# The experts of a mixture layer: every expert for every token, or tokens sorted by expert and gathered back

## The reference, cut to what matters

```python
xn = layernorm(x)
x = x + attn0(xn) + ffn0(xn)          # first layer
xn = layernorm(x)
x = x + attn1(xn) + ffn1(xn)          # second layer

def ffn0(u):                          # a mixture of experts
    s = softmax(u @ centroids.T + expert_biases)         # 16 experts
    topk_vals, topk_idx = top_k(s, 2)
    g = sum(one_hot(topk_idx, 16) * topk_vals)           # 2 of 16 not zero
    routed = sum over e of g[e] * (u @ Wr[e].T + br[e])   # Wr[e] is 256x256
    shared = (u @ (Ws[0] + Ws[1]).T + bs[0] + bs[1]) / 2
    return u + routed + shared
```

## Time and profile before

| | us |
|---|---|
| median of 3 runs (lowest, highest) | 3472.14 (3467.8, 3472.72) |
| the profiled execution, its own time | 3466.49 |
| its span, first to last instruction | 3464.7 |
| of it to the barrier between the phases | 1232.4 |
| of it `phase_b` | 2232.3 |

### The profile page before, as it was taken

One profiled execution on the slowest core, in us unless ns is written; L12 is line 12 of the kernel. 1 busy time (PEld: TensorE's weight loads), 2 busy tenths in 40 slices (PEclk: granted clock), 3 DMA queues, 4 the chain that ended last, 5 costly groups with the idle time before them and its releaser, 6 DMA issues.

```text
span 3464.7 us, 58322 instructions
## 1 busy us (share of the span) xinstructions
PE 3327.1 (96%) x16386; PEld 2701.4 (78%) x16386; DVE 2480.8 (72%) x4709; ACT 1951.3 (56%) x3226; POOL 2359.6 (68%) x2084
## 2 busy tenths in 40 slices
PE   5999999999999969999999999999999999999997
PEld 4877777777777747888888888888888888888886
DVE  6877777777777756766766667667677666776764
ACT  3333333333333347767767777677777777767774
POOL 4666666666666527777777777777777777777776
PEclk9999999999999979999999999999999999999999
DMA  2110011001001032222222222222322222222222
GB/s 78 31 31 28 28 31 31 26 29 31 27 29 31 25 94 59 47 71 63 59 71 56 62 70 50 66 70 46 74 59 59 73 56 60 70 50 66 70 49 53
DMA packets 195099, 180.22 MB, mean 52 GB/s; under 512 B 87955, under 2 KB 155813, under 8 KB 194469
## 3 DMA queue, kind: packets, MB, share of 16 engines
q1 hardware_dynamic: 194980, 179.04, 20.7%
HBM read 77.25 MB, written 34.08 MB: 32 GB/s over the span
## 4 chain that ended last, share of the span: by engine, by line
PE 61%; DMA 1%; ACT 1%; DVE 1%; POOL 1%; issue 0%; SPq 0%; POOLq 0%; ACTq 0%; DVEq 0%
PE psV_b L1342 7%; PE psV_b L1347 7%; PE psS_b L1330 7%; PE psS_b L1329 7%; PE psV_b L1343 7%; PE psN_b L1315 6%; PE psY_b L1270 4%; PE psX_b L1270 4%; PE psY_b L1271 3%; PE psY_b L1272 3%; PE psX_b L1272 3%; PE psX_b L1271 3%; POOL pp_lo_b L1061 1%; PE psN_b L1399 0%; DMA xT_lo<-xT_lo_dram 0%
## 5 line engine op out<-in xcount | busy, mean ns | idle before, releaser
L1061 POOL TENSOR_TENSOR pp_lo_b<-pf_b,pp_hi_b 128x1024 fp32r<-128x1024 f32 x512 | 1227.6, 2398 | 606.6 <-ACT pp_hi_b L1103 518.9
L1206 DVE TENSOR_REDUCE negmax_b<-psN_b 128x2 fp32r<-128x1024 f32 x512 | 627.1, 1225 | 387.8 <-PE psN_b L1315 380.1
L1098 ACT ACTIVATE pf_b<-psS_b 128x1024 f32<-128x1024 f32 x512 | 526.0, 1027 | 239.4 <-PE psS_b L1330 236.2
L692 PE MATMUL psM_a<-wr_hi_a,xt_hi_a 128*128 128x512 f32 x1024 | 439.6, 429 | 48.1 <-DVE acc_a L528 40.1
L1329 PE MATMUL psS_b<-qA_b,kA_b 128*128 128x512 f32 x1024 | 405.6, 396 | 6.3 <-DVE qB_b L1221 4.5
L694 PE MATMUL psM_a<-wr_hi_a,xt_lo_a 128*128 128x512 f32 x1024 | 409.7, 400 | 0.0
L693 PE MATMUL psM_a<-wr_lo_a,xt_hi_a 128*128 128x512 f32 x1024 | 407.8, 398 | 0.0
L1330 PE MATMUL psS_b<-qB_b,kB_b 68*128 68x512 f32 x1024 | 406.4, 397 | 0.0
L1342 PE MATMUL psV_b<-pp_hi_b,vals_hi_b 128*128 128x512 f32 x1024 | 402.9, 393 | 1.4
L1343 PE MATMUL psV_b<-pp_hi_b,vals_lo_b 128*128 128x512 f32 x1024 | 402.3, 393 | 0.0
L1315 PE MATMUL psN_b<-kA_b,qA_b 128*128 128x512 f32 x1024 | 322.8, 396 | 4.8 <-DVE negmax_b L1206 4.1
(11 more groups left out here) (200 smaller groups left out, 7824.1 us busy)
## 6 DMA issues: line engine op xcount, KB each, us to landing
kA_b<-kA_b SPq DMA_DIRECT2D x128, 256.0 KB, 3.2
qB_b<-qA_b SPq DMA_DIRECT2D x128, 256.0 KB, 2.9
inverse_b<-inverse_dram SPq DMA_DIRECT2D x256, 128.0 KB, 3.0
x_a<-x_dram SPq DMA_DIRECT2D x64, 128.0 KB, 2.1
xT_hi_dram<-xrt_hi_a SPq DMA_DIRECT2D x64, 128.0 KB, 2.1
xT_lo_dram<-xrt_lo_a SPq DMA_DIRECT2D x64, 128.0 KB, 2.1
base_dram<-base_a SPq DMA_DIRECT2D x64, 128.0 KB, 1.8
xT_hi<-xT_hi_dram SPq DMA_DIRECT2D x16, 512.0 KB, 4.3
```

The source lines that it names most:

```text
L692: pe.matmul(out, lh, rh, start=start, stop=False)
L1061: pool.tensor_tensor(pp[1][:, c], pf[:, c], pp[0][:, c].bitcast(F32), ALU.subtract).then_inc(pl_pool, 1)
L1098: a.activation(pf[:, c], psS[:], ACT.Exp).then_inc(exp_act, 1)
L1206: v.tensor_reduce(negmax[:, n.slot(2), 2 * c:2 * c + 2], psN[:], AX.X, ALU.max, negate=True).then_inc(mx_dve, 1)
```

## The change

`phase_a` is replaced by three blocks, one after the other, each closed by a barrier. Loops are written out; a unit is now two tiles (U = 2, 32 units), a group four tiles (16 groups). `need` is the wait.

`route`, 38 steps: normalization, routing, hidden layer and the shared expert, whose sum goes to DRAM (`part`). The experts are not multiplied. Instead DVE chooses two experts for each token of a group (`choose`: 15 operations over 4x16 numbers per token row, each waiting for the one before), TensorE counts with matmuls by triangular matrices how many earlier tokens chose the same expert, and DVE turns that into a row number (`settle_places`: 6 operations); `highest` is two more. POOL then writes each normalized tile twice to those rows of a DRAM array by indirect DMA: in every even step, 8 DMAs of 128 rows of 1 KB, in all 128. Every expert has a region of its own there. At the end SP loads 16 positions from SBUF into registers and writes zeros behind each region.

`experts`: 144 jobs of 128 rows, each of one expert, two per turn (72 turns). SP reads from a table where a job begins and loads the rows; TensorE transposes them, reads from the table which expert it is (`value_load`), and does 7 matmuls of 256 columns (one for the bias) with the weights at that place. ACT and DVE split the weights first, then the rows, and take turns in copying the results, which SP stores. POOL meanwhile converts the row numbers, in 30 small operations.

`settle`: per unit POOL gathers the two result rows of each token (4 indirect DMAs, three units ahead); DVE multiplies them by the two gates and adds them to `part`; then comes the second layer's normalization and ffn, and the stores as before.

```diff
+U = 2
+GU = TB // U
+TOP = 2
...
-def phase_a(nc, io, xT_hi, xT_lo, base_dram, early):
+def need(eng, sem, per, n, k):
+    if per * n + k > 0 and n >= 0:
+        eng.wait_ge(sem, per * n + k)
+def route(nc, io, rows, part, region, jobs, kept, raw, raw_in):
...
+        steps = range(-4, NU + 2)
...
+            sp.wait_ge(const_pool, POOL_CONST)
...
+            for r in range(4):
+                sp.wait_ge(sent[r], 16 * TOP * TB * (GN // 4))
+            for e in range(NE):
+                at = sp.value_load(ends_u[0:1, e:e + 1], min_val=0, max_val=NE * region - P)
+                sp.dma_start(rows[bass.ds(at, P), :], zeros[:]).then_inc(ends_in, 16)
...
+        @block.gpsimd
...
+            for v in steps:
+                u = v + 2
+                if 0 <= v < NU:
+                    hidden_low(v, 0)
+                if 0 <= u < NU:
+                    need(g, r_act, 3, u, 2)
+                    need(g, z_dve, 4, u - 2, 1)
+                    g.tensor_tensor(z2[:, u % 2], q2[:, u % 2], in_tiles(qw2_bc[:], U), ALU.mult).then_inc(z_pool, 1)
+                    g.tensor_tensor(sums[:, u % 4, :, FH:FH + 1], sums[:, u % 4, :, FH:FH + 1], eps[:, 4:4 + U].unsqueeze(2),
+                                    ALU.add).then_inc(z_pool, 1)
+                if v % 2 == 0 and 0 <= (v + 4) // 2 < GN:
...
+                    g.tensor_tensor(rstd[:, a % 2, 1], rstd[:, a % 2, 0], power[:, 0, 0:TB], ALU.pow).then_inc(ln_pool, 1)
+                if 0 <= v < NU:
+                    hidden_low(v, 1)
+                q = (v - 2) // 2
+                if v % 2 == 0 and 0 <= q < GN:
+                    need(g, rt_dve, ROUTE, q, ROUTE)
+                    for t in range(TB):
+                        for k in range(TOP):
+                            n = q * TB + t
+                            g.indirect_dma_start(out=rows[:, :], out_offset=bass.IndirectOffsetOnAxis(
+                                ap=kept.place[:, k, n:n + 1], axis=0), in_=xn[:, q % 4, t], in_offset=None).then_inc(sent[q % 4], 16)
+                if 0 <= u < NU:
+                    need(g, z_dve, 4, u, 1)
+                    need(g, z_dve, 4, u - 4, 3)
+                    need(g, z_pool, 3, u, 2)
+                    g.tensor_tensor(roots[:, u % 4].rearrange("p a b -> p (a b)"), sums[:, u % 4].rearrange("p a b -> p (a b)"),
+                                    power[:, 1, 0:U * (FH + 1)], ALU.pow).then_inc(z_pool, 1)
...
+        @block.scalar
...
+            for v in steps:
+                f1, f2, f3 = v + 1, v + 2, v + 3
+                if 0 <= v < NU:
+                    hidden_tanh(v, 0)
...
+                    a.activation(qsb[:, f2 % 2], psR[:, :, 0:D], ACT.Copy).then_inc(r_act, 1)
+                if 0 <= v < NU:
+                    hidden_high(v, 0)
+                if 0 <= f1 < NU:
...
+                    a.activation(qt[0][:, f1 % 2].rearrange("p a b c -> p (a b c)"), psQ[:, 0], ACT.Copy).then_inc(q_act, 1)
+                if 0 <= f3 < NU:
...
+                    a.activation(xt[0][:, f3 % 6].rearrange("p a b c -> p (a b c)"), psT[:, 0], ACT.Copy).then_inc(t_act, 1)
+                if 0 <= v < NU:
+                    hidden_tanh(v, 1)
+                    hidden_high(v, 1)
...
+        @block.vector
...
+            for s in steps:
+                f1, f2, f3 = s + 1, s + 2, s + 3
+                if 0 <= f1 < NU:
+                    need(v, z_pool, 3, f1, 3)
+                    root = roots[:, f1 % 4]
+                    v.scalar_tensor_tensor(out=qs[:, f1 % 4, 0], in0=root[:, :, FH:FH + 1].to_broadcast([P, U, FH]),
+                                           scalar=1e-5, in1=root[:, :, 0:FH], op0=ALU.mult, op1=ALU.add).then_inc(z_dve, 1)
+                    need(v, z_dve, 4, f1, 2)
...
+                    v.tensor_tensor(qn[:, f1 % 2].rearrange("p t (h d) -> p (t h) d", h=FH),
...
+                if 0 <= s < NU:
+                    hidden_product(s, 0)
+                if 0 <= f3 < NU:
+                    need(v, t_act, 1, f3, 1)
+                    v.tensor_tensor(xt[1][:, f3 % 6].rearrange("p a b c -> p (a b c)"), psT[:, 0],
...
+                    for t in range(TB):
+                        v.bn_stats(stats[:, g % 2, t], x[:, g % 4, t]).then_inc(ln_dve, 1)
...
+                        v.bn_aggr(mv[:, g % 2, t], stats[:, g % 2, t]).then_inc(ln_dve, 1)
...
+                    v.tensor_tensor(qt[1][:, f1 % 2].rearrange("p a b c -> p (a b c)"), psQ[:, 0],
...
+                    v.tensor_tensor(score[:, f2 // GU % 2, at:at + U], psR[:, :, D:D + NE], in_tiles(ebias_bc[:], U),
...
+                if s % 2 == 0 and 0 <= s // 2 < GN:
+                    choose(s // 2)
+                if s % 2 == 1 and 0 <= (s - 1) // 2 < GN:
+                    settle_places((s - 1) // 2)
+                if 0 <= s < NU:
+                    hidden_product(s, 1)
+                if 0 <= f2 < NU:
+                    need(v, z_pool, 3, f2, 1)
+                    v.tensor_reduce(sums[:, f2 % 4, :, 0:FH], z2[:, f2 % 2].rearrange("p t (h d) -> p t h d", h=FH), AX.X,
+                                    ALU.add).then_inc(z_dve, 1)
...
+                    v.tensor_tensor(acc[:, u % 2], psB[:, 0].rearrange("p (t n) -> p t n", t=U),
...
+                    highest(q)
...
+        @block.tensor
...
+                        for j in range(2):
+                            rows_j = slice(j * FD, (j + 1) * FD)
+                            mm = pe.matmul(psG[:, j, at:at + U * P], w[left][rows_j, p],
+                                           qt[right][rows_j, u % 2, p].rearrange("p a b -> p (a b)"),
+                                           start=(n == 0), stop=(n == 2))
...
+def experts(nc, io, rows, results, region, jobs, kept, raw, raw_in):
...
+        def where(eng, j):
+            return eng.value_load(kept.table[0:1, 2 * P + j:2 * P + j + 1], min_val=0, max_val=rows.shape[0] - P)
...
+                    sp.dma_start(xs[:, j % XS], rows[bass.ds(where(sp, j), P), :]).then_inc(x_in[j % XS], 16)
...
+                    at = pe.value_load(kept.table[0:1, j:j + 1], min_val=0, max_val=(NE - 1) * D)
+                    pe.matmul(out, kept.pick[:], brow[:, bass.ds(at, D)], start=True, stop=False)
+                    for k in range(KD):
+                        left = [part[:, n % 2, t, k] for part in xt]
+                        right = [part[:, k, bass.ds(at, D)] for part in wr]
+                        pe.matmul(out, left[0], right[0], start=False, stop=False)
+                        pe.matmul(out, left[0], right[1], start=False, stop=False)
+                        mm = pe.matmul(out, left[1], right[0], start=False, stop=(k == KD - 1))
...
+def settle(nc, io, results, part, xT_hi, xT_lo, base_dram, early, kept):
...
+            def gather(u):
+                if u < NU:
+                    need(g, s_dve, SD, u - 4, 4)
+                    for t in range(U):
+                        n = u * U + t
+                        for k in range(TOP):
+                            g.indirect_dma_start(out=y[:, u % 4, t, k], out_offset=None, in_=results[:, :],
+                                                 in_offset=bass.IndirectOffsetOnAxis(ap=kept.place[:, k, n:n + 1], axis=0)
+                                                 ).then_inc(y_in[u % 4], 16)
...
+            for u in range(NU):
+                need(g, s_dve, SD, u, 8)
...
+                g.tensor_tensor(root[:, u % 2, 0], vs[:, u % 2, 0], power[:, 0], ALU.pow).then_inc(s_pool, 1)
+                g.tensor_tensor(root[:, u % 2, 1], mv[:, u % 2, :, 1], power[:, 1], ALU.pow).then_inc(s_pool, 1)
...
+                g.tensor_tensor(x1b[:, u % 3], x1[:, u % 3], fbias_bc[:].unsqueeze(1).to_broadcast([P, U, D]),
...
+                gather(u + 3)
...
+            def finish(u):
...
+                need(v, f_pe, 1, u, 1)
+                for t in range(U):
+                    v.scalar_tensor_tensor(out=base[:, u % 2, t], in0=psF[:, u % 2, t * D:(t + 1) * D], scalar=fac[:, u % 3, 5, t:t + 1],
...
+                finish(u - 1)
+                f = fac[:, u % 3]
+                need(v, s_pool, SP, u, 3)
...
+    region = N + P
+    jobs = 2 * ((TOP * N + NE * (P - 1)) // P // 2 + 1)
...
-        phase_a(nc, io, xT_hi, xT_lo, base, early)
...
+                route(nc, io, rows, part, region, jobs, kept, raw, raw_in)
+                experts(nc, io, rows, results, region, jobs, kept, raw, raw_in)
+            settle(nc, io, results, part, xT_hi, xT_lo, base, early, kept)
```

More of the change, by code:

```diff
@@ new lines, in route @@
+        raw_b = sb("raw_b", [1, NS, D])
+        mean_s = sb("mean_s", [P, KD, D])
+        mean_b = sb("mean_b", [1, D])
+        tern = sb("tern", [P, 2, KD, D])
+        delta = sb("delta", [P, 4])
+        masks = sb("masks", [P, 4, P])
+        before = sb("before", [P, P], F32R)
+        behind = sb("behind", [P, P], F32R)
+        every = sb("every", [P, P], F32R)
+        zeros = sb("zeros", [P, D])
+        power = sb("power", [P, 2, 12])
+        eps = sb("eps", [P, 8])
```

(46 more changed lines are left out.)

1316 lines of the change are left out of this document (717 added, 599 removed).

## The result

The changed kernel takes 3544.19 us (median of 4 runs, 3540.79 to 3552.27), the kernel before 3472.43 in the same rounds: a ratio of 1.0213, 95% interval 1.0192 to 1.0233. It is slower, by 2.1%. I had forecast 3430 and faster; 3544 lies within the range given, which was wide enough for both signs.

A forecast was written before the change was run, and what follows sets the result against it. TensorE bounded the first phase before; after, POOL's chain in `route` and POOL in `settle`. `route` 686 + `experts` 236 + `settle` 271 = 1193 against 1232.4 us, 39 less: 3427 profiled, 3430 as median, range 3290 to 3590.

The forecast's parts named there:

- The chain: `route`, even step: eight scatters, then POOL's power for `roots`, for which DVE's next step waits; 28.9 + 8d per two steps.
- `experts` and `settle`: Forecast times of these two blocks: 236 us for `experts`, 271 us for `settle`, the latter bound narrowly by POOL.
- a turn of `experts`: `experts`: 3.0 us per turn, set by SP's and PE's queues, a `value_load` taken as 0.7 us.
- the walk of `route`'s step: `route`: one step walked through DVE, ACT and POOL; even step 16.5 + 8d, odd step ending at 12.4 us.
- TensorE's case: `route`: TensorE needs 9 us a unit, 18 us at most at the lower clock, and isn't what bounds the new blocks.
- PE under half busy in `route`: A sign to look for in the profile of `route`, beside even steps near 26 us and odd near 12.5.
- d: POOL's time for one indirect DMA: 1.2 us, ends 0.34 and 2.1; each 0.1 us moves the sum by 25 us.
- The beginning and end of `route`: `route` outside its loop: 44 us before it and 26 us after it.
- B: Rival for `route`'s even step and `settle`: dear descriptors, slower from 1.36 us on; at 1.8 us 3580 us; chance 0.18.
- C: Rival for `experts`: register loads and a cold TensorE, turns about 4.5 us, +108 us, 3538 us; chance 0.12.
- D: Rival for `settle`: a port lock, DVE's statistics hold up each unit's gathers, +96 us, 3526 us; chance 0.07.
- The floor of 0.6 us for a register load: `experts`: the Trainium skill's floor for a register load from memory; by it the sum would be 15 us lower.

The follow-up runs named there:

- e1: The changed kernel with the power `roots` moved ahead of the eight scatters in `route`; 3379.5 us, ratio to the kernel before 0.9732.
- e10: The changed kernel with 18 of the 38 psB matmuls of each `route` step left out; 3479.5 us.
- e4: The changed kernel with scatters as plain SP DMAs, fixed addresses in `experts`, `x1b` off GpSimd in `settle`; `route` 636.0 us, `experts` 188.0 us.
- e3: The changed kernel with 16384 instead of 1024 bytes for descriptors, `phase_b` left out; a group 46.1 us, `route` 10 us shorter.
- e8: On e5, in `settle`, `x1b` moved to VectorE and `base` behind the next unit's factors; a unit from 8.10 to 7.14 us.
- e7: The changed kernel with 36 extra filler matmuls in each odd step of `route` and TensorE's addresses fixed in `experts`; 3533.4 us.
- e6: On e5, the eight scatters of a group split into four in each step; 3338.8 us.
- e5: On e1, psC's matmuls issued later in `route`; 3366.4 us.

## Why the prediction was wrong

The chain, the step on which it rested, was right: VectorE idles 13.8 to 14.7 us behind `roots` (10 to 12 forecast), and e1 takes 155 us off. `experts` and `settle` were right within 5%, though in `settle` the bound was two loops, not GpSimd alone. That a turn of `experts` came out at 3.04 where 3.0 stood is in part luck: the turn without any load is 2.35 us, not 2.1, and the four loads together cost 0.7, where a single one had been put at 0.7.

**The step that failed** is the walk of `route`'s step with the three other engines only, and the sentence before it that closed TensorE's case: 9 us of work a unit, 18 at most at the lower clock, against steps of 26 and 12.4. The 18 was longer than the odd step of 12.4 to which it had to be held. The walk then gives TensorE 18 us in two steps, which is the 9 of the full clock twice; two steps at the lower clock would be 36 of the 38.5. The trace has TensorE at the lower clock through much of `route` (0.62), psR, psQ, psT standing ahead of ACT's `xt_hi` in the even step, and psB, behind psC's stop, ahead of VectorE's `acc` in the odd one. With it the odd step is 14.9 to 17.7 us, shorter where the clock rises within psB, and in the even step it adds the 2.1 us of `xt_hi`. e10 confirms it by taking work away: with 18 matmuls less in each step the group is 3.87 us shorter. e4 shows the same waits and a floor of 17.7 without any scatter. The forecast's own sign, PE under half busy in `route`, failed too: it was busy for 455.7 of 790.8 us, 58%.

**A term mis-sized:** d measured 1.46 where 1.2 was taken. By its own working, 16 x 8 x 0.26 = 33 us in `route` and 0.05 x 4 x 32 = 6 in `settle`, where the pitch was 1.25. Most of the excess is the eighth's 2.0 us, and e3 shows that taking it away returns only 10 us of `route`, since TensorE's floor comes next. The sum of the miss: a group is 8.3 us too long, 133 us in 16; of it d is 2.1, and the other 6.2, some 100 us, stand in the waits for psB, psR and psG, TensorE's; e10 gave back 57 of it by taking half of psB away. The beginning and end of `route` took 28 us less than forecast (42 where 70 stood), which hid a part of it.

Of the rivals, B (dear descriptors) named the right sign, and d was above its 1.36; but by the forecast's own slope 1.46 in both stages is +65 us, 3495, and with the 1.25 measured in `settle` +39, 3469, not 3544. C didn't come: TensorE's clock was 0.94 in `experts`. D: gathers in `settle` took 0.94 to 1.16 us and seldom more in e8, with more VectorE work beside them. The rule that the forecast took from the Trainium skill, SBUF — State Buffer, section SBUF: two separate sides, speaks of VectorE operations that use both ports; no such hold shows in these rows, and whether any operation of `settle` is of that kind no run here shows. The floor of 0.6 us for a register load in the Trainium skill, DMA: Bandwidth & Descriptors, section Latency and other measured facts, isn't contradicted: what shows is 0.50 us a turn for two of SP's loads and 0.19 for TensorE's two. How long a single load takes no run here shows.

## What to carry to other kernels

When an engine loses its work, don't leave it out of the walk: compare its time at the lower clock with each step, the shortest first, and look for where its results are waited for. Descriptor writing on GpSimd belongs behind whatever the next step waits for on that engine; here the order of two statements was worth 155 us, twice what the change had lost. And a stage with two loops of equal length gave 5 us when one was cut and 31 when both were.

## What the runs showed of the hardware

An indirect DMA of 128 rows of 1 KB holds GpSimd for 0.97 us, 1.27 us from start to start, in either direction; with 1024 bytes for descriptors the eighth of a burst waits 1.7 to 2.5 us in the changed kernel, where the others wait 0.3, with 16384 bytes not. I had not expected that after a filled gap the clock is down again behind 3.0 us of idle (e7). And VectorE's operations can be held by GpSimd's: in e6, VectorE and then GpSimd,

```profile
307.33 0.18 DVE L506 RECIPROCAL small_a<-small_a 128x4 f32<-128x4 f32 x1
307.54 1.70 DVE L507 TENSOR_TENSOR prob_a<-expo_a,small_a 128x64 f32<-128x64 f32 x1
309.27 0.22 DVE L508 TENSOR_REDUCE share<-prob_a 128x4 f32<-128x64 f32 x1
```

```profile
306.65 1.27 POOL L316 TENSOR_TENSOR hd_lo_a<-th_a,hd_hi_a 128x512 fp32r<-128x512 f32 x1
307.89 1.25 POOL L326 TENSOR_TENSOR z_a<-q_a,qw_bc_a 128x512 f32<-128x512 f32 x1
```

an operation of 0.23 us in the changed kernel takes 1.70 and ends 0.1 us after z2 does. The same stands in all eleven groups of the loop, with 1.70 to 2.95 us; in e5, where only GpSimd's short power of 128x4 runs beside it, it takes 0.23. VectorE's busy time for eleven groups rose from 220 us (e5) to 258 (e6), 20 of it in L507 and 14 in L529 (the `place` work), so shortening VectorE's waits had its price in longer operations. No run tests this apart.
